# Cross-attention block with FFN on one core: the order of V's split and the softmax in the last step of an iteration

## The reference

```
q = ln(x) @ w_q.T          # 32 heads of 32
k = ctx @ w_k.T            # 8 groups of 32, 4 heads share one
v = ctx @ w_v.T            # 8 groups of 32
p = softmax(where(mask, q k^T / sqrt(32), -max))
x = x + (p @ v) @ w_out.T
h = ln(x) @ w12.T + b12    # two halves of 1024, x1 and x2
x = x + (silu(x1) * x2) @ w3.T + b3
```

## Time and profile before

| what | value |
|---|---|
| three runs | 1115.85, 1118.41, 1118.98 us; median 1118.41 |
| the profiled execution's own time | 1119.04 us |
| its span in the profile | 1117.3 us |
| TensorE busy, share of the span | 97% |
| VectorE, ScalarE, GpSimd busy | 51%, 38%, 35% |
| mean granted TensorE clock | 0.987 of full |

### The profile page before, as it was taken

One profiled execution on the slowest core, in us unless ns is written; L12 is line 12 of the kernel. 1 busy time (PEld: TensorE's weight loads), 2 busy tenths in 40 slices (PEclk: granted clock), 3 DMA queues, 4 the chain that ended last, 5 costly groups with the idle time before them and its releaser, 6 DMA issues.

```text
span 1117.3 us, 19426 instructions
## 1 busy us (share of the span) xinstructions
PE 1079.1 (97%) x7952; PEld 658.4 (59%) x7952; DVE 571.1 (51%) x1062; ACT 425.3 (38%) x899; POOL 392.8 (35%) x376
## 2 busy tenths in 40 slices
PE   8887999999999989999999999999999999999998
PEld 7776766767768667676655544444444444444443
DVE  6869776776776766577755322631134111431121
ACT  6757555555656455455566520111110111011100
POOL 2769801613315224157686688112000300121000
PEclk8999899999999999999999999999999999999999
DMA  9657597996988858569793644370006300360001
GB/s 367 213 145 169 134 255 191 204 230 165 251 195 213 208 173 210 121 172 232 183 243 81 175 160 159 71 241 1 1 4 151 147 1 1 76 188 1 1 1 76
DMA packets 201512, 162.24 MB, mean 145 GB/s; under 512 B 162640, under 2 KB 172880, under 8 KB 196560
## 3 DMA queue, kind: packets, MB, share of 16 engines
q1 hardware_dynamic: 201424, 161.01, 54.3%
HBM read 93.87 MB, written 27.26 MB: 108 GB/s over the span
## 4 chain that ended last, share of the span: by engine, by line
PE 75%; DVE 11%; ACT 4%; DMA 2%; issue 1%; POOL 1%; SPq 0%; DVEq 0%; ACTq 0%
PE bank_dense L984 69%; ACT arena_attn L816 2%; DVE arena_in L1356 2%; DMA arena_attn<-arena_attn 2%; PE bank_score L1045 1%; PE bank_score L1041 1%; DVE arena_rows L1328 1%; DVE arena_in L1359 1%; DVE arena_in L1269 1%; DVE arena_rows L1317 1%; PE bank_dense L1001 1%; PE bank_av L1063 1%; PE bank_av L1067 1%; DVE arena_in L1373 1%; PE bank_av L1065 1%
## 5 line engine op out<-in xcount | busy, mean ns | idle before, releaser
L984 PE MATMUL bank_dense<-arena_rows,arena_in 128*128 128x256 f16 (+1 forms) x2304 | 348.1, 309 | 3.6 <-DVE small L1231 1.4
L984 PEld LDWEIGHTS bank_dense<-arena_rows,arena_in 128*128 128x128 f16 x2304 | 224.3, 98 | 111.3 <-DVE small L1231 1.7
L816 ACT ACTIVATE arena_attn<-bank_score,arena_in 128x128 f32<-128x128 f32 x512 | 192.9, 467 | 160.6 <-DVE arena_in L1359 160.6
L984 PE MATMUL bank_dense<-arena_out,arena_attn 128*128 128x512 f16 x768 | 170.5, 379 | 0.0
L984 PE MATMUL bank_dense<-arena_out,arena_in 128*128 128x512 f16 x768 | 166.1, 379 | 0.9 <-issue 0.9
L984 PE MATMUL bank_dense<-arena_attn,arena_rows 128*128 128x512 f16 x768 | 166.4, 379 | 0.0
L1408 DVE SCALAR_TENSOR_TENSOR arena_attn<-bank_dense,small,arena_attn 128x512 f32<-128x512 f32 x32 | 24.0, 751 | 221.3 <-PE bank_dense L984 221.3
L702 POOL TENSOR_TENSOR arena_attn<-arena_attn 128x512 f16<-128x512 f32 x53 | 62.6, 1181 | 199.3 <-ACT arena_attn L825 199.3
L984 PEld LDWEIGHTS bank_dense<-arena_out,arena_in 128*128 128x128 f16 x768 | 75.1, 98 | 91.7 <-issue 1.5
L984 PEld LDWEIGHTS bank_dense<-arena_attn,arena_rows 128*128 128x128 f16 x768 | 75.1, 98 | 90.6
L658 POOL TENSOR_TENSOR small<-small 128x1 f32<-128x1 f32 x32 | 24.1, 755 | 289.7 <-DVE small L1311 289.6
(11 more groups left out here) (124 smaller groups left out, 1326.1 us busy)
## 6 DMA issues: line engine op xcount, KB each, us to landing
arena_rows<-x SPq DMA_DIRECT2D x32, 512.0 KB, 6.0
arena_attn<-q_scratch SPq DMA_DIRECT2D x48, 256.0 KB, 4.6
arena_rows<-w_t SPq DMA_DIRECT2D x12, 1024.0 KB, 6.1
arena_rows<-ctx_t SPq DMA_DIRECT2D x8, 1024.0 KB, 5.9
q_scratch<-arena_attn SPq DMA_DIRECT2D x16, 512.0 KB, 5.2
x_scratch<-arena_rows SPq DMA_DIRECT2D x16, 512.0 KB, 3.9
arena_out<-x_scratch SPq DMA_DIRECT2D x16, 512.0 KB, 6.0
out<-arena_out SPq DMA_DIRECT2D x16, 512.0 KB, 3.8
```

Source lines behind the costliest of these rows:

```text
L816: ins = act.activation(e[:, g % 2, u, SEQ * j:SEQ * j + SEQ], B_SCORE[g % 2][:, SEQ * h:SEQ * h + SEQ], ACT.Exp, bias=neg_max[:, g % 2, h: ...
L984: ins = pe.matmul(dst, lhs(a, c), rhs(b, c), start=(c == 0 and n == 0), stop=(c == KC - 1 and n == 2))
```

## The change

In step 7 of iterations 2 to 7, six steps in all, ScalarE does `v_hi(t, 0)` ahead of the first four exponentials instead of behind them, and VectorE does `v_lo(t, 0)` ahead of `prob_lo(g-1)` instead of behind it. The order on TensorE, GpSimd and SyncE, the order of the banks and the counts of all semaphores stay. Iterations 1 and 8 stay as they are (in 8 there is no V).

```diff
@@ -906,6 +906,9 @@
             for t in range(1, NB + 1):
                 for s in range(STEPS):
                     g, (tile, tile2) = GROUPS * (t - 1) + s, x_tiles(t, s)
+                    v_first = 1 < t < NB and s == LAST
+                    if v_first:
+                        v_hi(t, 0)
                     exps(g, 0)
                     if t == NB and s - 1 in H_AT:
                         hid_hi(0, H_AT[s - 1])
@@ -915,7 +918,8 @@
                         silus(0, H_AT[s])
                         attn_hi(g - 3)
                         continue
-                    unit_hi(first_unit(t, s))
+                    if not v_first:
+                        unit_hi(first_unit(t, s))
                     if tile is not None:
                         x_hi(tile, 0)
                         x_hi(tile, 1)
@@ -1530,9 +1534,13 @@
                         hid_lo(0, H_AT[s - 1])
                     if name:
                         gather_top(name)
-                    if g >= 1:
+                    if 1 < t < NB and s == LAST:
+                        v_lo(t, 0)
                         prob_lo(g - 1)
-                    unit_lo(first_unit(t, s))
+                    else:
+                        if g >= 1:
+                            prob_lo(g - 1)
+                        unit_lo(first_unit(t, s))
                     if tile is not None:
                         x_lo(tile, 0)
                         x_lo(tile, 1)
```

## The result

| | before | after |
|---|---|---|
| median of 20 runs each | 1117.78 us | 1122.09 us |
| lowest and highest | 1109.40, 1122.64 | 1118.83, 1129.51 |
| profiled execution: own time, span | 1119.04, 1117.3 us | 1126.96, 1125.2 us |
| mean granted clock in it | 0.987 | 0.987 |
| ratio after to before | | 1.0056, 95% interval 1.0038 to 1.0073 |

The change makes the kernel slower by 0.4 to 0.7%. The lines of the changed kernel lie up to four further down from the diff's second part on: L977, L984, L1001, L1328 and L1333 are now L981, L988, L1005, L1332 and L1337.

A forecast was written before the change was run, and what follows sets the result against it. TensorE, busy 97% of the span, was taken to set the end. From the profiled 1119.04 us, 3.8 for the reordering and 3.3 for the clock gave 1126.2, or 1125.5 on the median; range 1121.0 to 1129.5.

The forecast's parts named there:

- The binding wait: Step 7, before V unit 1: the x tile's second low part is the last read, so `x_hi`'s start on ScalarE matters.
- The size of the exchange: ScalarE waits for V unit 0 in six steps: 4 x 0.60 + 1.21 + 0.23 = 3.84 us lost on TensorE.
- the wake-up after V unit 0: ScalarE's `v_hi` was to start 2.82 us after V unit 0 began, product and wake-up together.
- The hand-over from `v_hi` to an exponential: On ScalarE, taken as 0.26 us; waiting for `v_hi`'s end would add at most 0.16 a step, 1.0 in all.
- The waits: TensorE, iterations 2 to 6: `spread`'s wait goes; `turn_attn` waits about 1.9 us, its group growing from 2.3 to some 10.
- The transpose of P: SyncE issues it at about 190.5 instead of 189.82; it lands after 1.85 us and the delay costs nothing.
- The clock: V unit 1's product falls to half clock in two more steps, 3.3 us; bounds none more (or -3.3) and 6.7.
- the four of six: Count of V unit 1 products expected at half clock, taken between two and six: two more, 3.3 us.
- longer is worse: TensorE's wait ahead of V unit 1: about 2 us doesn't decide alone, but longer idleness makes half clock likelier.
- rival (a): Loss as summed, half clock no more often: 1122.2 us, or 1120.5 with one stretch fewer; chance 0.20.
- Nothing gives it back: After iteration 7 TensorE's stream is nearly without waits, so nothing later recovers the loss.
- What a measurement can tell: Whole kernel: a difference of 0.3%, 3.4 us, is about what can be told from no change.

The follow-up runs named there:

- e3: Changed kernel with V's first high part behind two of the four exponentials on ScalarE, VectorE as changed; ratio to the kernel before 1.0012 (0.9985 to 1.0038).
- e1: Changed kernel with VectorE's exchange undone, so only ScalarE's exchange remains; ratio to the kernel before 1.0051 (1.0032 to 1.0070).
- e5: Changed kernel plus 14 idle transposes in TensorE's wait ahead of `turn_attn`, six steps; ratio to the kernel before 1.0032 (1.0014 to 1.0050).
- e6: Kernel before plus 8 idle transposes in TensorE's wait ahead of `spread`, iterations 2 to 6; ratio to the kernel before 0.9977 (0.9963 to 0.9992).
- e4: Changed kernel with x's high parts also ahead of the exponentials, its low parts ahead of P's low part; ratio to the kernel before 0.9959 (0.9943 to 0.9975).
- e8: e4 with iteration 1 changed in the same way; ratio to the kernel before 0.9947 (0.9925 to 0.9970), on another chip than e4.
- e0_same: The kernel before, unedited, measured against itself; ratio 0.9995 (0.9977 to 1.0012).

## Why the prediction was right

**The binding wait.** It said that three reads must be over before V unit 1 and that the last is the x tile's second low part, so V's earlier read wins nothing. e3 shows it: V read early, V unit 1 not a hundredth earlier in iterations 2 to 5. The wait of `spread` was large in the list because it is the first of three in a row, not because it decides.

**The size of the exchange.** Forecast 3.84 us, measured 4.17. In iterations 2 to 5 0.65 or 0.66 a step against 0.60: the wake-up after V unit 0 took 2.88 us from its start, not 2.82. The hand-over from `v_hi` to an exponential was 0.28, the value taken was 0.26, the upper bound 0.42. Iterations 6 and 7 were 1.26 and 0.28 against 1.21 and 0.23; that iteration 7 fits is partly luck, since it moves by 0.37 between two traces of the kernel before.

**The waits.** Forecast: none left for V's low part and one of 1.9 us for the x tile, some 10 us in total. Measured: 0.21, 1.80 and 9.0.

**The transpose of P.** The prediction has it land 1.85 us after its issue. That is a misreading, and the text ahead of it has the same: the length of a DMA's row in the timeline is the time that its issue takes on the queue, not the time to its landing. The transpose issued at 189.82 landed 4.3 us later, and over the kernel before the 64 transposes of P took 4.2 to 9.6 us. In this step the conclusion stands all the same: with the change it was issued 4.35 us after V unit 0 began, where it was 3.71 (0.64 later; forecast 0.65), and P times V started 8.6 us after the landing in both. In other steps the margin is smaller, 0.1 to 0.4 us for group 16.

**The clock** is the term that was mis-sized. I took two more slow products, 3.3 us. The trace has one more, not at full length: 1.3 us. The traces alone don't even show the direction, since both of the kernel before have two of six, the changed kernel's three and e1's, with waits as long, two. Over the runs, the mean clock was 0.9891 in the 20 runs of the changed kernel and 0.9906 in 35 of the kernel before, which ran beside the experiments; at 0.7 to 1.0 us for each 0.001, that is an estimate of 1.1 to 1.5 us. e1's 12 runs, which stood beside those 35, have 0.9884. So the direction was right and the size about half of what I took. e5 and e6 show the cause; the four of six that I chose between two and six had no better ground than the middle, and "longer is worse" was an assumption, which the traces bear out only between waits of 0.7 us in all (none of 12 slow in e4 and e8) and of 1.2 us and more. With one in place of two the sum gives 1123.9 on the median; the measured 1122.09 is 1.8 below (and 3.4 below the forecast's own 1125.5), and the ratio, which compares all runs, would put it at 1.0056 x 1117.78 = 1124.0. By its median alone the result is that of rival (a), 1122.2, the loss without any more slow products; only the mean clock and the ratio speak against it, so between the forecast and that rival the time doesn't decide.

By the rule of the Trainium skill ("TensorE: Matmul & The Clock Gate", Why this matters for your kernels) none of the gaps in these steps was long enough to bring the clock down. The trace shows a wait of 1.80 us followed by a product of 4.46 in iterations 5 and 6, and e5 and e6 that the slow products go when the wait is filled; here the measurement decides.

**Nothing gives it back**, as forecast: from V unit 1 of iteration 7 to the end the two spans differ by 0.2 us (563.99 and 563.80).

**What a measurement can tell.** The prediction took 0.3%. The intervals of the result and of e0_same are 0.2% wide to either side, so a change of 0.6% is clear.

## What to carry to other kernels

When an engine's instruction waits for one of several reads in a row, ask which of them is over last before the next long piece of work; making the first one earlier only lengthens the wait for the last. Before an in-order engine's block is put ahead of another, compare when the inputs of the two are ready: a block that must wait holds up everything queued behind it, by the difference of the two times (0.66 and 1.26 us here). If a block is to come forward, bring forward what the bound engine really waits for, as e4 did, and let the work that nobody waits for come last. And don't read the length of a DMA's row as its time to landing: ask for the landing.

## What the runs showed of the hardware

A TensorE wait of 1.8 us can be followed by a product that takes 4.46 us instead of 2.79: in the changed kernel's trace three of six such products were slow (4.05, 4.46 and 4.46 us), in e1's, with waits of 1.5 to 1.8, two (4.33 and 4.17). Fourteen idle float32 transposes of 128x128 in that wait (1.75 us) went with a granted clock of 1.00 through all six steps. Eight of them (1.04 us) ahead of `spread` made the unchanged kernel 0.2% faster (0.9963 to 0.9992), though they add work and take none away: filling a wait with work that nobody reads paid by itself, if little more than these runs can tell.

A DMA transpose of P took 4.2 to 9.6 us from its issue to its landing in one trace of the kernel before, and the same transpose, that of group 16, 7.2 and 7.4 us in the two traces of that kernel and 9.0 to 9.7 in the nine of the others.
